# Expert stage: outputs copied by mask in place of masked relu rows, and the last projection placed between the last recurrence steps

## The reference, cut to what matters

```python
# recurrence output h2: (batch, 126, 256); its projection is added to the stream
h = h + einsum('bth,ho->bto', h2, Wfc) + bfc
# second expert stage, on x = layernorm(h)
idx = argmax(x @ Wg + bg)                # one expert of 8 for each token
out = 0
for e in range(8):
    hid = relu(x @ W1[e] + b1[e])        # 128 -> 256
    y   = hid @ W2[e] + b2[e]            # 256 -> 128
    out = where(idx == e, y, out)
h = h + out
```

## Time and profile before

| what | us |
|---|---|
| median of the three runs | 1154.62 |
| lowest, highest | 1150.05, 1154.71 |
| the profiled execution's own time | 1148.86 |
| its span, first to last instruction | 1147.1 |
| mean granted clock of TensorE | 0.91 of full |
| TensorE busy | 911.7 (79%) |
| VectorE busy | 838.3 (73%) |
| ScalarE busy | 626.5 (55%) |
| GpSimd busy | 346.5 (30%) |

### The profile page before, as it was taken

How to read it: one execution, slowest core, us unless ns; L and a number is a source line. 1 busy time by engine, 2 the same in 40 slices (tenths; PEclk the granted TensorE clock), 3 DMA queues, 4 the chain that set the end, 5 groups by cost and what they waited for, 6 DMA issues and landing times.

```text
span 1147.1 us, 44853 instructions
## 1 busy us (share of the span) xinstructions
PE 911.7 (79%) x17506; PEld 715.0 (62%) x17506; DVE 838.3 (73%) x2903; ACT 626.5 (55%) x1954; POOL 346.5 (30%) x479
## 2 busy tenths in 40 slices
PE   3757777168787777865699999999999999679897
PEld 1345545035555454532599899899899899546665
DVE  3558986986666666657688888888888888556998
ACT  0547777136666665643455555555555555335775
POOL 0326755866566556530000000000100000011221
PEclk9779997569999999986699999999999999778999
DMA  8600023202221221224000000000000000003231
GB/s 249 241 1 1 1 83 112 59 27 63 63 63 63 63 63 37 39 73 124 3 4 0 0 0 0 0 0 0 0 0 0 0 0 0 2 1 129 91 110 52
DMA packets 26712, 52.13 MB, mean 45 GB/s; under 512 B 4528, under 2 KB 17816, under 8 KB 26648
## 3 DMA queue, kind: packets, MB, share of 16 engines
q1 hardware_dynamic: 21656, 41.04, 10.9%
q0 software_dynamic: 4992, 10.23, 3.4%
HBM read 44.02 MB, written 7.24 MB: 45 GB/s over the span
## 4 chain that ended last, share of the span: by engine, by line
PE 29%; DVE 14%; issue 11%; ACT 0%; DVEq 0%; POOL 0%; DMA 0%; POOLq 0%
PE quad L1322 18%; PE bank L1322 7%; DVE hidL L1701 4%; DVE post L1461 3%; DVE post L1497 2%; DVE area L1715 2%; DVE post L1503 1%; DVE post L1498 1%; PE quad L1382 1%; PE quad L1332 1%; PE bank L1617 1%; PE quad L1606 1%; PE bank L1611 0%; PE bank L339 0%; DVE area L376 0%
## 5 line engine op out<-in xcount | busy, mean ns | idle before, releaser
L1322 PE MATMUL quad<-post,area 128*128 128x32 f16 (+1 forms) x7520 | 231.1, 182 | 28.1 <-DVE post L1503 21.5
L1322 PEld LDWEIGHTS quad<-post,area 128*128 128x128 f16 x7520 | 213.9, 97 | 43.0 <-DVE post L1503 42.9
L1322 PE MATMUL bank<-post,area 128*128 128x32 f16 (+1 forms) x6260 | 193.3, 180 | 7.0 <-DVE post L1503 4.8
L1322 PEld LDWEIGHTS bank<-post,area 128*128 128x128 f16 x6260 | 176.9, 96 | 12.7 <-DVE post L1503 5.3
L1400 ACT ACTIVATE post<-post 128x64 f32<-128x64 f32 x252 | 64.6, 256 | 159.1 <-DVE post L1461 159.1
L1305 POOL COPY post<-post 128x32 f32 (+1 forms) x126 | 26.5, 210 | 382.6 <-DVE post L1503 382.6
L846 POOL DMA_INDIRECT y_scratch<-area x78 | 84.5, 1084 | 82.3 <-DVE area L1206 68.4
L1487 DVE SCALAR_TENSOR_TENSOR post<-post 128x32 f32<-128x32 f32 x252 | 48.5, 193 | 75.2 <-ACT post L1411 75.2
L927 PE MATMUL quad<-const,area 128*128 128x128 f16 x624 | 55.5, 222 | 47.6 <-DVE area L1193 32.3
L927 PEld LDWEIGHTS quad<-const,area 128*128 128x128 f16 x624 | 40.1, 99 | 79.7 <-DVE area L1193 39.2
L841 POOL DMA_INDIRECT area<-x_scratch,area x78 | 79.2, 1015 | 27.6 <-issue 22.5
(11 more groups left out here) (254 smaller groups left out, 2122.6 us busy)
## 6 DMA issues: line engine op xcount, KB each, us to landing
w0s<-in_w SPq DMA_DIRECT2D x12, 768.0 KB, 12.5
area<-mask_scratch SPq DMA_DIRECT2D x7, 1008.0 KB, 4.8
area<-in_rec SPq DMA_DIRECT2D x7, 640.0 KB
post<-y_scratch SPq DMA_DIRECT2D x16, 252.0 KB
area<-in_w SPq DMA_DIRECT2D x4, 768.0 KB
post<-in_f SPq DMA_DIRECT2D x8, 256.0 KB, 4.7
area<-in_patches SPq DMA_DIRECT2D x1, 1488.4 KB
area<-in_taps SPq DMA_DIRECT2D x1, 1350.0 KB
```

The costliest lines, as they stand in the source:

```text
L1322: mm = pe.matmul(at[0][:, at[1] + out.start:at[1] + out.stop], rec_w[:, w, s, m * P:(m + 1) * P], operand, start=False, stop=False, skip_g ...
```

## The change

There are three parts.

1. *Expert stage.* The mask multiply and `fhid` are gone. `high` and `low` read `relu` itself. A block's downs start a new sum in bank j for each expert (`start=c == 0`) and end it. `pick_own` then copies, by predicate, those columns of bank j whose token has chosen this expert into `xn_blocks[j]`. Blocks 0 and 1 are copied at items 5 and 7 of the same expert, blocks 2 and 3 at items 1 and 3 of the next; within the loop a tiny memset stands ahead of each copy. `finish` adds `xn` to the stream at the end. The waits on `masked` become waits on `f_hid_low` (ScalarE's relu) and `picked` (SyncE's mask loads and the first down of a block).
2. *Order at the start.* Transposes, mask rows and b2 matmuls move from ahead of expert 0 to behind its third up; VectorE adds the four b2 banks to the stream at once.
3. *Projection.* `connect` runs blocks 0 to 2 on TensorE behind steps t = 125, 127, 128 and 129 of the wave (`FC_AFTER`; SEQ is 126), in banks 2, 3 and 0; block 3 follows the wave, in bank 1. Norm ln4 uses banks 2, 3, 0, 1 and 4 (`LN4_BANKS`).

```diff
-        fhid = view(2 * BLK).rearrange("p (u n) -> p u n", u=2)
+        warm_dve = view(8)[0:1, 0:1]
...
+        FC_BANK = (2, 3, 0, 1)
+        FC_AFTER = {SEQ - 1: ((0, 0),), SEQ + 1: ((0, 1),), SEQ + 2: ((1, 0), (1, 1)), SEQ + 3: ((2, 0), (2, 1))}
...
+            def connect(j, k):
+                if k == 0:
+                    pe.wait_ge(sg("fcw_in"), 16)
+                    pe.wait_ge(sg("hist"), ((j + 1) * BLK + BATCH - 1) // BATCH)
+                    pe.wait_ge(sg("sum_x0"), SEQ - 2 if j < 2 else SEQ)
+                    pe.wait_ge(sg("sum_y0"), SEQ - 2 if j < 2 else SEQ)
+                mm = pe.matmul(bank[FC_BANK[j]][:, 0:BLK], fc_w[:, k, :],
+                               blk(hist_k[:, k].rearrange("p t b -> p (t b)"), j),
+                               start=(k == 0), stop=(k == KH - 1))
+                if k == KH - 1:
+                    mm.then_inc(sg("fc"), 1)
...
+                for j, k in FC_AFTER.get(t, ()) if isinstance(t, int) else ():
+                    connect(j, k)
             wave(pe, both)
-            pe.wait_ge(sg("fcw_in"), 16)
-            pe.wait_ge(sg("hist"), SEQ)
-            for j in range(NBLK):
-                for k in range(KH):
-                    mm = pe.matmul(bank[4 + j][:, 0:BLK], fc_w[:, k, :],
-                                   blk(hist_k[:, k].rearrange("p t b -> p (t b)"), j),
-                                   start=(k == 0), stop=(k == KH - 1))
-                mm.then_inc(sg("fc"), 1)
+            for k in range(KH):
+                connect(NBLK - 1, k)
...
+        LN4_BANKS = [bank[i] for i in (*FC_BANK, 4)]
...
-                    sp.wait_ge(sg("masked"), (e - 1) * ITEMS1)
+                    sp.wait_ge(sg("picked"), e * NBLK)
...
+            def turn_mask():
+                pe.wait_ge(sg("mask"), 1)
+                for t in range(TILES):
+                    mm = pe.transpose(bank[t // 4][0:E1, t % 4 * SEQ:(t % 4 + 1) * SEQ], chosen[:, t],
+                                      ident[0:SEQ, 0:SEQ])
+                    if t % 4 == 3:
+                        mm.then_inc(sg("mask_ps"), 1)
+                for j in range(NBLK):
+                    pe.wait_ge(sg("mask_T"), j + 1)
+                    pe.matmul(bank[j][:, 0:BLK], fb2, blk(mask_T, j), start=True, stop=True, skip_group_check=True
+                              ).then_inc(sg("mask_ps"), 1)
+            def down(e, k, u):
                 j, c = divmod(k, C1)
+                n = e * ITEMS1 + k
                 w = H1 + c * P
+                if c == 0:
+                    pe.wait_ge(sg("picked"), e * NBLK + j + 1)
                 pe.wait_ge(sg("f_hid_low"), n + 1)
                 split3(pe, bank[j][:, 0:BLK], wH[:, u, w:w + P], wL[:, u, w:w + P], hidH[:, k % 4, :],
-                       hidL[:, k % 4, :], start=False, stop=False).then_inc(sg("f_down"), 1)
+                       hidL[:, k % 4, :], start=c == 0, stop=c == C1 - 1).then_inc(sg("f_down"), 1)
             def expert(e, u, half):
                 first = isinstance(e, int) and e == 0
                 for k in range(ITEMS1):
                     j, c = divmod(k, C1)
                     n = e * ITEMS1 + k
+                    if first and k == LAG:
+                        turn_mask()
...
+            def mask_rows():
+                for j in range(NBLK):
+                    act.wait_ge(sg("mask_ps"), j + 1)
+                    act.activation(blk(mask_T, j), bank[j][0:E1, 0:BLK], ACT.Copy).then_inc(sg("mask_T"), 1)
             def high(n, k):
-                act.wait_ge(sg("masked"), n + 1)
+                act.wait_ge(sg("relu"), n + 1)
                 if not isinstance(n, int) or n >= 4:
                     act.wait_ge(sg("f_down"), n - 3)
-                act.activation(hidH[:, k % 4, :], fhid[:, k % 2, :], ACT.Copy).then_inc(sg("f_hid_high"), 1)
+                act.activation(hidH[:, k % 4, :], relu[:, k % 2, :], ACT.Copy).then_inc(sg("f_hid_high"), 1)
...
+                    if first and k == LAG:
+                        mask_rows()
                     act.wait_ge(sg("f_up"), n + 1)
                     if not (first and k < 2):
-                        act.wait_ge(sg("masked"), n - 1)
+                        act.wait_ge(sg("f_hid_low"), n - 1)
                     act.activation(relu[:, k % 2, :], bank[4 + k % 4][:, 0:BLK], ACT.Relu,
...
-                dve.tensor_tensor(hidL[:, k % 4, :], fhid[:, k % 2, :], hidH[:, k % 4, :].bitcast(F32), ALU.subtract
+                dve.tensor_tensor(hidL[:, k % 4, :], relu[:, k % 2, :], hidH[:, k % 4, :].bitcast(F32), ALU.subtract
                                   ).then_inc(sg("f_hid_low"), 1)
+            def pick_own(e, j, u, half):
+                if isinstance(e, int) and e == 0 and j == 0:
+                    dve.wait_ge(sg("mask_first"), 16)
+                elif j == (1 if isinstance(e, int) and e == 0 else 0):
+                    dve.wait_ge(sg(f"mask_in{u}"), half * 16 + 16)
+                dve.wait_ge(sg("f_down"), e * ITEMS1 + (j + 1) * C1)
+                if not isinstance(e, int):
+                    dve.memset(warm_dve, 0.0)
+                dve.copy_predicated(xn_blocks[j], blk(mask_b[:, u], j).bitcast(I32), bank[j][:, 0:BLK]
+                                    ).then_inc(sg("picked"), 1)
+            def finish(j):
+                dve.wait_ge(sg("picked"), E1 * NBLK + j + 1)
+                dve.tensor_tensor(st_blocks[j], st_blocks[j], xn_blocks[j], ALU.add).then_inc(sg("final"), 1)
             def expert(e, u, half):
-                first = isinstance(e, int) and e == 0
+                first, last = isinstance(e, int) and e == 0, isinstance(e, int) and e == E1 - 1
                 for k in range(ITEMS1):
                     n = e * ITEMS1 + k
-                    if first and k == 0:
-                        dve.wait_ge(sg("mask_first"), 16)
-                    if k == (C1 if first else 0):
-                        dve.wait_ge(sg(f"mask_in{u}"), half * 16 + 16)
-                    dve.wait_ge(sg("relu"), n + 1)
-                    if not (first and k < 2):
-                        dve.wait_ge(sg("f_hid_low"), n - 1)
-                    dve.tensor_tensor(fhid[:, k % 2, :], relu[:, k % 2, :], blk(mask_b[:, u], k // C1), ALU.mult
-                                      ).then_inc(sg("masked"), 1)
+                    if first and k == LAG:
+                        for j in range(NBLK):
+                            dve.wait_ge(sg("mask_ps"), NBLK + j + 1)
+                            dve.tensor_tensor(st_blocks[j], st_blocks[j], bank[j][:, 0:BLK], ALU.add
+                                              ).then_inc(sg("picked"), 1)
                     if not (first and k == 0):
                         low(n - 1, (k - 1) % ITEMS1)
+                    if k in (5, 7):
+                        pick_own(e, (k - 5) // 2, u, half)
+                        if last:
+                            finish((k - 5) // 2)
+                    if k in (1, 3) and not first:
+                        pick_own(e - 1, (k + 3) // 2, 1 - u, half + u - 1)
             experts(expert)(dve, E1)
             low(E1 * ITEMS1 - 1, ITEMS1 - 1)
-            dve.wait_ge(sg("f_down"), E1 * ITEMS1)
-            for j in range(NBLK):
-                dve.tensor_tensor(st_blocks[j], st_blocks[j], bank[j][:, 0:BLK], ALU.add).then_inc(sg("final"), 1)
+            for j in range(NBLK // 2, NBLK):
+                pick_own(E1 - 1, j, 1, E1 // 2 - 1)
+                finish(j)
```

More of the change, by code:

```diff
@@ L1424, in rec_act @@
                     act.wait_ge(sg("recurred"), j - 1)
-                act.activation(fc_sb[:, j % 2], bank[4 + j][:, 0:BLK], ACT.Identity, bias=col(FC_B),
+                act.activation(fc_sb[:, j % 2], bank[FC_BANK[j]][:, 0:BLK], ACT.Identity, bias=col(FC_B),
                                scale=1.0 / H_SCALE).then_inc(sg("fc_sb"), 1)
@@ L1601, in last_pe @@
         def last_pe(pe):
-            norm_pe(pe, "ln4", st_blocks, bank, lambda e, j: e.wait_ge(sg("recurred"), j + 1))
+            norm_pe(pe, "ln4", st_blocks, LN4_BANKS, lambda e, j: e.wait_ge(sg("recurred"), j + 1))
             pe.wait_ge(sg("fg_in"), 48)
@@ L1608, in last_pe @@
             mm.then_inc(sg("f_logits"), 1)
[L1609 to L1614, removed]
-            for j in range(NBLK):
-                pe.wait_ge(sg("mask_T"), j + 1)
-                pe.matmul(bank[j][:, 0:BLK], fb2, blk(mask_T, j), start=True, stop=False, skip_group_check=True)
-            def down(n, k, u):
+            def turn_mask():
[10 more added lines that the diff above has]
+            def down(e, k, u):
                 j, c = divmod(k, C1)
+                n = e * ITEMS1 + k
                 w = H1 + c * P
+                if c == 0:
+                    pe.wait_ge(sg("picked"), e * NBLK + j + 1)
                 pe.wait_ge(sg("f_hid_low"), n + 1)
                 split3(pe, bank[j][:, 0:BLK], wH[:, u, w:w + P], wL[:, u, w:w + P], hidH[:, k % 4, :],
```

(23 more changed lines are left out.)

## The result

The changed kernel took 1177.12 us, the median of four runs (1171.52 to 1181.22), against 1154.66 for the kernel before on the same chip (four runs, 1150.05 to 1159.83). The ratio is 1.0197, 95% interval 1.017 to 1.0223: 2% slower. The forecast was 1178.

What follows compares the result with a forecast made beforehand. VectorE, with TensorE right behind, was taken to bound the expert stage at 1.38 us an item. Terms +24.1 + 7.2 - 0.3 - 6.0 - 0.8 = +24.2 us gave 1178 us, range 1160 to 1198.

Steps and rivals of the forecast that it cites:

- What decides the stage: Expert stage: relu is held until the low half reads it, putting relu, high and low in series; +24.1 us.
- The size of an item: Expert stage: one item takes 0.58 + 0.62 + 0.68 + 0.09 = 1.97 us; 58 items 114.3 us against 90.15.
- GpSimd's splits: Expert stage: GpSimd's weight splits delay VectorE's low halves or copies, 1.2 us for each of six experts: +7.2 us (0 to 15.6).
- The copies: Expert stage: predicated copies, 0.68 us plus about 0.1 for the memset, fit VectorE's 1.29 us pause: hidden, 0 us.
- Rival 3: Expert stage: a copy costs more than the pause, above 2 us with its switches; +25 us, 1203; chance 0.05.
- Start of the stage: Logits to relu(5): early ups fill a pause, winning two microseconds nearly all lost to filling the serial cycle: -0.3 us.
- Projection: Last recurrence steps to the means: six of eight projection matmuls move into TensorE's pauses; -6.0 us, bounds -7.1 and +0.9.
- End: From relu(63) to the end: 8.2 us in place of 9.5, -1.3; -0.8 with the last expert's adds and rounding.
- Total: Whole kernel: the steps sum to +24.2 us, span 1147.1 to 1171.3; median forecast 1178.
- rival 2: Expert stage: TensorE's clock falls in the gaps, +0.65 us per affected item; half of them +21 us, 1199; chance 0.10.
- The signs: Expert stage trace: relu to relu 1.9 to 2.0 us, wait on low half, VectorE busy 60 to 70%, expert 15.8 to 17 us.

Runs made afterwards that it cites:

- small split: Changed kernel with GpSimd splitting 8 of 512 columns of each weight from expert 2 on: 1163.09 us against 1154.14 for the kernel before; relu(5) to relu(63) 115.91 us.
- second profile of the changed kernel: Changed kernel unaltered, run again beside the kernel before on another chip: 1121.46 us against 1101.82, ratio 1.017; logits to relu(5) 23.85 us.
- projection alone: Kernel before with only the projection part of the change (connect between the last steps, its banks and the norm's): 1094.35 us against 1103.49, ratio 0.9932.
- two runs above: Kernel before with only the projection part, 1094.35 us; changed kernel with transposes, mask rows and b2 matmuls back ahead of the first up, 1125.92 us; both against 1103.49.
- two variants of the kernel before: Kernel before with relu(n) also waiting for low(n-2), 1196.12 us against 1154.14; kernel before with ScalarE issuing relu(n), high(n), 1137.89 us against 1101.82.
- late release: Kernel before with one added wait, relu(n) waiting for low(n-2): 1196.12 us against 1154.14; relu(5) to relu(63) 128.8 us.

## Why the prediction came out right, step by step

- *What decides the stage.* Right, and shown from four sides. More buffers or another order take the whole loss away with every copy in place, doubled copies don't add to it, and one wait brings it into the kernel before.
- *The size of an item.* 1.97 us forecast, 2.00 measured; the two hand-overs come to 0.13 and not 0.09 (the prediction takes 0.05 for each and adds 0.09). Over 58 items, without the splits (115.91 in the small split), that is 1.6 us more than the 114.3 of the sum.
- *GpSimd's splits.* 7.2 us forecast, 4.1 measured by the small split. The forecast had 0.8 us an expert for the first pass and 0.4 for the second. The first pass does cover the start of one low half by 0.82 us (1082.78 to 1083.60), and that costs 0.67. The second costs VectorE nothing. The sum of 4.8, by the Trainium skill ("SBUF — State Buffer", section "SBUF: two separate sides") for a copy that escapes the lock, was nearer. The rows agree with it: the copy of 1084.07 is 0.73 us long in the middle of GpSimd's second pass of 1083.68, while the low half before it was held up by the first. The second pass began under that low half and took 1.61 us itself in place of the 1.28 of the earlier trace rows.
- *The copies.* 0.68 us plus 0.1 for the memset forecast, 0.72 measured, with the memset's 0.06 inside the same stretch; hidden, as forecast. Rival 3, dear copies, is out with it.
- *Start of the stage.* This step was mis-sized: -0.3 us forecast, -4.6 measured (-3.6 in the second profile of the changed kernel), at the end of the bound given there (up to 4 us more if the clock rises). The clock did rise at the third up, so the transposes took 1.88 us, and the b2 matmuls 3.87 in place of 7.08. The first is part 2's work and the second mostly part 3's, by the projection alone. The cost of filling the serial cycle, which the forecast set against them at nearly 2 us, is there too: 2.9 us by the two runs above.
- *Projection.* -6.0 net forecast. From the last `own` to the means it is -6.6, and 0.3 was lost in the delayed steps: -6.3 net. The clock stayed at 1.00 until 993.1 us, 6.5 us behind the start of step 125 at 986.62, and was back by 996.6; before it fell 3.2 us behind that start (982.4 and 985.6) and stayed low into the projection. The forecast had not seen that, and so the last steps were hardly late.
- *End.* -1.2 forecast, -0.1 measured. The forecast missed that the copy and the final add of block 1 (item 7) stand ahead of the last low half on VectorE, which so starts 1.3 us later, and the last down ran at half clock, 1.6 us in place of 1.0:

```profile
1161.51 0.68 DVE L1727 TENSOR_TENSOR hidL<-area,hidH 128x504 fp32r<-128x504 f32 x1 [1.32 <-ACT hidH L1684]
1162.11 0.72 DVE L1739 COPY_PREDICATED xn<-area,bank 128x504 f32<-128x504 int32 x1
1162.86 0.68 DVE L1744 TENSOR_TENSOR stream<-stream,xn 128x504 f32<-128x504 f32 x1
1163.47 0.68 DVE L1727 TENSOR_TENSOR hidL<-area,hidH 128x504 fp32r<-128x504 f32 x1
...
1165.86 0.72 DVE L1739 COPY_PREDICATED xn<-area,bank 128x504 f32<-128x504 int32 x1 [0.37 <-PE bank L320]
```

- *Total.* +24.2 forecast. The tail gave +18.4, and on the other chip +19.6 in the whole. In the pair of profiled executions another 4 us came from the first expert stage, which scattered by as much between executions; the +22.5 of the medians most likely owes as much to it, though the other runs have no profile that could show it. So the hit on 1178 is in part luck: the large shares are right in sign and order, and the sum was about 5 us too high.
- *The clock in the gaps* (rival 2) did not fall in the changed kernel: 1.00 over 105 us with TensorE busy 79% by these records. It is a real risk all the same: in the two variants of the kernel before with items of about 2 us it fell to 0.50 behind seven of twelve splits, for some 3 us each. With the late release no item was longer for it.
- *The signs.* An expert takes 16.65 us (15.8 to 17 forecast) and the wait before relu is on the low half. VectorE is busy 52% of the stage and not 60 to 70: eight low halves, four copies and 0.67 us for the split are 9.0 of 16.65 us. That number of the forecast did not follow from its own terms either.

## What to carry to other kernels

When a tile between two stages goes, look at who releases the tile that takes over its role, and write down the cycle of waits from one use of the buffer to the next, with each engine's program order in it: a chain that crosses two engines and comes back within one item bounds the pace whatever the busy shares say. Two engines that wait for each other about equally often, neither of them full, are its sign in a profile. Before adding buffers, try the order: issuing the operation that frees the buffer earlier was worth 41 us here, without one more buffer, and the same order was wrong by 31 us in the kernel that had one more operation of VectorE between the two.

## What the runs showed of the hardware that I had not expected

- Two groups of chips: the kernel before took 1154 us on one and 1102 to 1103 on the other. The difference lies in the first expert stage, with its 156 indirect DMAs: the gathers run from 239.0 to 487.2 us on one and, in the changed kernel, from 239.1 to 440.4 on the other. For the changed kernel each stretch of the table from the last `own` on agrees within 1 us. Why the gathers differ is open.
- The clock at the b2 matmuls depended on the projection some 30 us earlier (7.08 us three times of three with the old projection, 3.64 to 4.45 nine times of nine with the new), although it was at half in between in both. In eight of the nine they took at most 4.02; the 4.45 is the run with four relu buffers, in which the transposes took 2.95 us, not the 1.88 or 1.89 of the six others that have part 2.
- A predicated copy of 128x504 from PSUM under a mask in SBUF took 0.72 us, 0.04 more than an add of that size, and 0.73 beside a pass of GpSimd that held up a low half before it.
